# The mask phase of a two-layer cross-attention kernel with each chunk attended directly ahead of the next chunk's scores

## The reference

```python
xq = layer_norm(x, qn_w, qn_b)
ctx = layer_norm(context, cn_w, cn_b)
q = (xq @ q_w).reshape(B, N, H, D)               # H = 16 heads of D = 32
kv = (ctx @ kv_w).reshape(B, M, 2, H, D)
k, v = (kv[:, :, 0], kv[:, :, 1])
attn = jnp.einsum('bnhd,bmhd->bhnm', q, k) * scale
attn = jnp.where(xa_mask[:, None, :, :], neg, attn)
attn = jax.nn.softmax(attn, axis=-1)
out = jnp.einsum('bhnm,bmhd->bnhd', attn, v).reshape(B, N, C)
x = x + (out @ proj_w + proj_b)
```

## Time and profile before

| what | us |
|---|---|
| runs of the kernel before | median 2971.13 (2970.61 to 2973.69, 3 runs) |
| the profiled execution's own time | 2967.99 |
| its span, first to last instruction | 2965.3 |
| PE busy | 2803.9 (95%) |
| DVE busy | 1747.2 (59%) |
| ACT busy | 1632.9 (55%) |
| POOL busy | 631.0 (21%) |
| mean granted clock of PE | 0.980 of full |

### The profile page before, as it was taken

How to read it: one execution, slowest core, us unless ns; L and a number is a source line. 1 busy time by engine, 2 the same in 40 slices (tenths; PEclk the granted TensorE clock), 3 DMA queues, 4 the chain that set the end, 5 groups by cost and what they waited for, 6 DMA issues and landing times. The chain is left out here.

```text
span 2965.3 us, 69016 instructions
## 1 busy us (share of the span) xinstructions
PE 2803.9 (95%) x24864; PEld 2430.4 (82%) x24864; DVE 1747.2 (59%) x5357; ACT 1632.9 (55%) x4947; POOL 631.0 (21%) x773
## 2 busy tenths in 40 slices
PE   6999999996999999999899999995999999999995
PEld 6888888885888888888699998994888888888884
DVE  6666666664533332333367777775576767767674
ACT  6777777774311111111177777774666656656562
POOL 1110111021000000000012333332133324333233
PEclk9999999999999999999899999997999999999998
DMA  3111101111200000000211111113110011110100
GB/s 114 43 45 58 58 29 58 58 43 68 100 29 29 28 14 14 28 28 14 78 35 45 42 42 42 42 57 115 47 43 35 35 42 42 42 35 35 42 29 22
DMA packets 74804, 134.37 MB, mean 45 GB/s; under 512 B 10096, under 2 KB 10096, under 8 KB 74736
## 3 DMA queue, kind: packets, MB, share of 16 engines
q1 hardware_dynamic: 74736, 133.47, 13.0%
HBM read 99.90 MB, written 33.55 MB: 45 GB/s over the span
## 5 line engine op out<-in xcount | busy, mean ns | idle before, releaser
L1967 ACT ACTIVATE mlp_h<-mlp_f,mlp_b1col 128x512 f32<-128x512 f32 x128 | 88.3, 690 | 559.4 <-PE mlp_f L2091 559.3
L2027 DVE CAST mlp_hT_hi<-mlp_h 128x512 fp32r<-128x512 f32 x128 | 58.3, 455 | 440.0 <-ACT mlp_h L1967 440.0
L519 ACT ACTIVATE cross_prob<-cross_scores,cross_low 128x256 f32<-128x256 f32 x512 | 237.9, 492 | 14.1 <-DVE cross_low L897 14.1
L519 ACT ACTIVATE mask_prob<-mask_scores,mask_low 128x256 f32<-128x256 f32 x512 | 236.8, 475 | 11.3 <-DVE mask_low L903 10.3
L903 DVE CUSTOM_DVE_ANT_0 mask_scores<-mask_scores,mask_mask 128x256 f32<-128x256 f32 x512 | 201.5, 456 | 69.2 <-PE mask_scores L1296 68.7
L519 ACT ACTIVATE causal_prob<-causal_scores,causal_low 128x128 f32<-128x128 f32 (+1 forms) x512 | 211.1, 434 | 15.4 <-DVE causal_low L903 15.3
L2091 PE MATMUL mlp_f<-mlp_xT_hi,mlp_w_hi 128*128 128x512 f32 x512 | 200.2, 391 | 0.6 <-DVE mlp_xT_lo L2021 0.6
L2103 PE MATMUL mlp_acc<-mlp_w_hi,mlp_hT_hi 128*128 128x512 f32 x512 | 200.6, 392 | 0.0
L2091 PE MATMUL mlp_f<-mlp_xT_hi,mlp_w_lo 128*128 128x512 f32 x512 | 199.9, 391 | 0.0
L2091 PE MATMUL mlp_f<-mlp_xT_lo,mlp_w_hi 128*128 128x512 f32 x512 | 199.9, 390 | 0.0
L2103 PE MATMUL mlp_acc<-mlp_w_hi,mlp_hT_lo 128*128 128x512 f32 x512 | 199.4, 389 | 0.0
(11 more groups left out here) (333 smaller groups left out, 9394.4 us busy)
## 6 DMA issues: line engine op xcount, KB each, us to landing
mask_x_in<-in_x SPq DMA_DIRECT2D x16, 512.0 KB, 3.7
mask_c_in<-in_ctx SPq DMA_DIRECT2D x16, 512.0 KB, 5.2
mask_res<-in_x SPq DMA_DIRECT2D x16, 512.0 KB, 3.5
after_attention<-mask_res SPq DMA_DIRECT2D x16, 512.0 KB, 5.9
mlp_x<-after_attention SPq DMA_DIRECT2D x8, 1024.0 KB, 5.6
mlp_stage<-in_L_xattn_fc_w SPq DMA_DIRECT2D x8, 1024.0 KB, 5.0
after_layer<-mlp_y SPq DMA_DIRECT2D x8, 1024.0 KB, 4.2
causal_x_in<-after_layer SPq DMA_DIRECT2D x16, 512.0 KB, 4.1
```

The source lines that it names most:

```text
L519: ins = act.activation(prob[:, u % 4, qt, 0:w], SC[h][:, FROM[qt]:FROM[qt] + w], ACT.Exp, bias=low[:, u % 4, qt:qt + 1], scale=-1.0, accum ...
L1967: act.activation(h32[:, m % 2, :], F1[m % 2][:], ACT.Gelu, bias=b1col[:, m:m + 1]).then_inc(s["gelu"], 1)
L2027: dve.tensor_copy(hT[0][:, r, :], h32[:, r, :]).then_inc(s["h_hi"], 1)
```

## The change

It changes the order of the instructions in the mask phase on PE, ACT and DVE. Head 3 of a chunk is turned ahead of the second keys block (no longer in halves), `attend` follows keys and stands directly ahead of the next `scores`, and `attended` and the first turn of the new chunk follow the first block behind scores. Each later turn moves up by one block. In chunk 2 both `turn_over` calls stand together ahead of `queries(b + 1, 0)`. ACT's exponentials of a chunk and DVE's minima are no longer split by another instruction. `post_turn` of the second pair goes into SC[2] in place of O, so it waits for the exponentials of head 2, and scores wait for `post_lo`. The fourth matrix is split in turn 0 rather than in the prologue, and `qk_lo(b, 1)` on DVE goes to the end of the turn before. Twelve columns of indentation are taken off; "..." stands for chunk 3 of PE's turn, which follows the pattern of chunk 1 with the values of b+1 in place of the projection: attended(b, 2) and turn 12 behind the first half, then turn 13, queries half, turn 14, queries half, `post_turn(b, 0)`.

```diff
@@ -196,7 +196,7 @@
 T_BANK = (W1, O) if causal else (SC[2], SC[3], SC[2], SC[3])
 QK_BANK = W1 if cross else W0
 V_BANK = W0 if cross else W1
-POST_BANK = (W1, O) if cross else (SC[2], O)
+POST_BANK = (W1, O) if cross else (SC[2], SC[2])
 PT_BANK = (SC[0], SC[1], PT, PT)
@@ -567,42 +567,38 @@
 def mask_turn(b, prev, cur, nxt):
     if prev:
-        copy(b, -1)
-    if cur:
-        for u in (0, 1, 2):
+        attended(b, -1)
+    if cur:
+        for u in (0, 1, 2, 3):
             exps(b, u)
-    if prev:
-        attended(b, -1)
-    if cur:
-        exps(b, 3)
-        values(b, 1)
         copy(b, 0)
         copy(b, 1)
+        copy(b, 2)
     if prev:
         post_hi(b, 1)
-    if cur:
-        copy(b, 2)
+    elif cur:
+        matrix_hi(3)
+    if cur:
+        values(b, 1)
+        copy(b, 3)
         qk(b, 2)
-        copy(b, 3)
-        for u in (4, 5, 6):
+        attended(b, 0)
+        for u in (4, 5, 6, 7):
             exps(b, u)
-        attended(b, 0)
-        exps(b, 7)
         copy(b, 4)
         copy(b, 5)
+        copy(b, 6)
     if nxt:
         turned(b + 1, 0)
         turned(b + 1, 1)
     if cur:
-        copy(b, 6)
+        copy(b, 7)
         qk(b, 3)
-        copy(b, 7)
-        for u in (8, 9, 10):
+        attended(b, 1)
+        for u in (8, 9, 10, 11):
             exps(b, u)
-        attended(b, 1)
-        exps(b, 11)
         copy(b, 8)
     if nxt:
         turned(b + 1, 2)
@@ -610,22 +606,22 @@
     if cur:
         copy(b, 9)
         copy(b, 10)
+        copy(b, 11)
     if nxt:
         qk(b + 1, 0)
     if cur:
-        copy(b, 11)
-        for u in (12, 13, 14):
+        attended(b, 2)
+        for u in (12, 13, 14, 15):
             exps(b, u)
-        attended(b, 2)
-        exps(b, 15)
-    if nxt:
-        values(b + 1, 0)
-    if cur:
         copy(b, 12)
         copy(b, 13)
+        copy(b, 14)
+    if nxt:
+        values(b + 1, 0)
+    if cur:
         post_hi(b + 1, 0)
-        copy(b, 14)
+        copy(b, 15)
     if nxt:
         qk(b + 1, 1)
@@ -771,7 +767,6 @@
     matrix_hi(2)
     qk(0, 0)
     values(0, 0)
-    matrix_hi(3)
     qk(0, 1)
@@ -1014,51 +1009,48 @@
 def mask_turn(b, prev, cur, nxt):
     if cur:
-        minima(b, 0, (0, 1))
-        qk_lo(b, 1)
-        minima(b, 0, (2, 3))
+        minima(b, 0)
     if prev:
         attended(b, -1)
     if nxt:
         front(b + 1)
     if prev:
         post_lo(b, 1)
-    if cur:
-        minima(b, 1, (0, 1))
+    elif cur:
+        matrix_lo(3)
+    if cur:
         qk_lo(b, 2)
-        minima(b, 1, (2, 3))
+    if cur:
+        minima(b, 1)
+        attended(b, 0)
     if prev:
         project(b, 0)
-    if cur:
-        attended(b, 0)
     if nxt:
         turned(b + 1, 0)
         turned(b + 1, 1)
-    if cur:
-        minima(b, 2, (0, 1))
+    if cur:
         qk_lo(b, 3)
-        minima(b, 2, (2, 3))
+    if cur:
+        minima(b, 2)
+        attended(b, 1)
     if prev:
         project(b, 1)
     if nxt:
         turned(b + 1, 2)
         turned(b + 1, 3)
-    if cur:
-        attended(b, 1)
-    if cur:
-        minima(b, 3, (0, 1))
-    if nxt:
         qk_lo(b + 1, 0)
-    if cur:
-        minima(b, 3, (2, 3))
+    if cur:
+        minima(b, 3)
+        attended(b, 2)
     if nxt:
         mask_floats(b + 1)
     if cur:
-        attended(b, 2)
         post_lo(b + 1, 0)
+    if nxt:
+        qk_lo(b + 1, 1)
@@ -1192,7 +1184,7 @@
     matrix_lo(2)
     qk_lo(0, 0)
     mask_floats(0)
-    matrix_lo(3)
+    qk_lo(0, 1)
@@ -1406,145 +1398,122 @@
         if prev:
             pe.wait_ge(s["post_lo"], 2 * (b - 1) + 1)
         scores(b, 0)
-    if prev:
-        turn_probs(b, -1)
-    if cur:
         pe.wait_ge(s["v_ready"], 2 * b + 1)
         values(b, 1, 0)
-    if prev:
-        attend(b, -1)
-    if cur:
+    if prev:
+        attended(b, -1)
+    if cur:
+        turn_probs(b, 0)
         values(b, 1, 1)
-        turn_probs(b, 0)
-    if prev:
-        attended(b, -1)
-    if cur:
+        turn_probs(b, 1)
         pe.wait_ge(s["qk_lo"], KC * b + 2)
         queries(b, 2, 0)
-        turn_probs(b, 1)
+        turn_probs(b, 2)
         queries(b, 2, 1)
     if prev:
         pe.wait_ge(s["z_done"], KC * b + 1)
+        if cur:
+            scores_taken(b, 2)
         post_turn(b - 1, 1)
     if cur:
-        keys(b, 2, 0)
-        turned_free(b, 0)
-        turn_probs(b, 2)
-        keys(b, 2, 1)
+        turn_probs(b, 3)
+        keys(b, 2)
+        attend(b, 0)
+    if prev:
+        pe.wait_ge(s["post_lo"], 2 * b)
     if cur:
         scores(b, 1)
-        turn_probs(b, 3)
-    if prev:
-        pe.wait_ge(s["post_lo"], 2 * b)
+    if prev:
         pe.wait_ge(s["v_ready"], 2 * b + 2 if cur else 2 * B)
         project(b, 0, 0)
-    if cur:
-        attend(b, 0)
+    if cur:
+        attended(b, 0)
+        turn_probs(b, 4)
     if prev:
         project(b, 0, 1)
     if cur:
-        turn_probs(b, 4)
-    if cur:
-        attended(b, 0)
+        turn_probs(b, 5)
         pe.wait_ge(s["qk_lo"], KC * b + 3)
         queries(b, 3, 0)
-        turn_probs(b, 5)
+        turn_probs(b, 6)
         queries(b, 3, 1)
     if nxt:
         scores_taken(b, 6)
         turn_over(b + 1, 0)
         scores_taken(b, 7)
         turn_over(b + 1, 1)
     if cur:
-        keys(b, 3, 0)
-        turned_free(b, 1)
-        turn_probs(b, 6)
-        keys(b, 3, 1)
+        turn_probs(b, 7)
+        keys(b, 3)
+        attend(b, 1)
     if cur:
         if nxt:
             pe.wait_ge(s["t_act"], NP * (b + 1) + 2)
         scores(b, 2)
-        turn_probs(b, 7)
     if prev:
         pe.wait_ge(s["proj_read"], TT * (b - 1) + 2)
         project(b, 1, 0)
-    if cur:
-        attend(b, 1)
+    if cur:
+        attended(b, 1)
+        turn_probs(b, 8)
     if prev:
         project(b, 1, 1)
     if cur:
-        turn_probs(b, 8)
+        turn_probs(b, 9)
     if nxt:
         scores_taken(b, 10)
         turn_over(b + 1, 2)
+        scores_taken(b, 11)
+        turn_over(b + 1, 3)
+    if cur:
+        turn_probs(b, 10)
+    if nxt:
         pe.wait_ge(s["qk_lo"], KC * (b + 1))
         pe.wait_ge(s["t_lo"], NP * (b + 1) + 2)
         queries(b + 1, 0)
-        scores_taken(b, 11)
-        turn_over(b + 1, 3)
-    if cur:
-        turn_probs(b, 9)
-    if cur:
-        attended(b, 1)
+    if cur:
+        turn_probs(b, 11)
     if nxt:
         pe.wait_ge(s["t_lo"], NP * (b + 1) + 3)
         keys(b + 1, 0, 0)
-    if cur:
-        turned_free(b, 2)
-        turn_probs(b, 10)
-    if nxt:
         pe.wait_ge(s["t_lo"], NP * (b + 2))
         keys(b + 1, 0, 1)
+    if cur:
+        attend(b, 2)
...
-    if nxt:
-        keys(b + 1, 1, 0)
-    if cur:
-        turned_free(b, 3)
-        turn_probs(b, 14)
-    if nxt:
-        keys(b + 1, 1, 1)
+        turn_probs(b, 15)
+    if nxt:
+        keys(b + 1, 1)
+    if cur:
+        attend(b, 3)
```

More of the change, by code:

```diff
@@ L569, in mask_turn @@
                 if prev:
-                    copy(b, -1)
-                if cur:
-                    for u in (0, 1, 2):
-                        exps(b, u)
-                if prev:
                     attended(b, -1)
                 if cur:
-                    exps(b, 3)
-                    values(b, 1)
+                    for u in (0, 1, 2, 3):
+                        exps(b, u)
                     copy(b, 0)
                     copy(b, 1)
+                    copy(b, 2)
                 if prev:
                     post_hi(b, 1)
+                elif cur:
+                    matrix_hi(3)
                 if cur:
-                    copy(b, 2)
+                    values(b, 1)
+                    copy(b, 3)
                     qk(b, 2)
-                    copy(b, 3)
-                    for u in (4, 5, 6):
+                    attended(b, 0)
+                    for u in (4, 5, 6, 7):
                         exps(b, u)
-                    attended(b, 0)
-                    exps(b, 7)
                     copy(b, 4)
                     copy(b, 5)
+                    copy(b, 6)
                 if nxt:
@@ L616, in mask_turn @@
                 if cur:
-                    copy(b, 11)
-                    for u in (12, 13, 14):
+                    attended(b, 2)
+                    for u in (12, 13, 14, 15):
                         exps(b, u)
-                    attended(b, 2)
-                    exps(b, 15)
+                    copy(b, 12)
+                    copy(b, 13)
+                    copy(b, 14)
                 if nxt:
@@ L624, in mask_turn @@
                 if cur:
-                    copy(b, 12)
-                    copy(b, 13)
                     post_hi(b + 1, 0)
-                    copy(b, 14)
+                    copy(b, 15)
                 if nxt:
@@ L1415, in mask_turn @@
                 if prev:
-                    attend(b, -1)
-                if cur:
-                    values(b, 1, 1)
-                    turn_probs(b, 0)
-                if prev:
                     attended(b, -1)
```

(17 more changed lines are left out.)

## The result

| | before | after |
|---|---|---|
| median of 4 runs each, us | 2971.51 (2970.61 to 2973.69) | 3015.76 (3010.89 to 3016.80) |
| ratio | | 1.0145, interval 1.0127 to 1.0162 |
| profiled execution, us | 2967.99 | 3016.80 |
| its span, mean granted clock | 2965.3, 0.980 | 3014.9, 0.977 |

The change makes the kernel 1.5% slower. The forecast was 3008 us, range 2987 to 3024.

What follows compares the result with a forecast made beforehand. PE's own instruction order was taken to set the time (busy 42.78 of 43.00 us a turn). Loop 30.1, turn 0 5.0 and the end 1.9 summed to +37 us on the median 2971.13: 3008 us, range 2987 to 3024.

Steps and rivals of the forecast that it cites:

- (a): PE, each chunk: one change of array shape less, four to three; 0.15 us gained, 10 over 64 chunks.
- the unshown price: PE, attend directly followed by scores: taken as 1.00 us, bounds 0.11 less and 0.21 more.
- the walk: PE's instruction prices added through the new chunk 0 without any wait: 10.24 us against 10.39 before.
- (b): First turn of every chunk, 2.66 us behind scores, needs exponentials ready at 3.17: PE waits 0.51 us.
- The rival in which the gain comes through: First turn finds its exponentials ready, or waits were already counted: 1.3 us a turn gained, 2956 us; 7%.
- ACT's order: ACT's queued copies come late: attend in chunk 1 waits 0.35 us, turn 11 in chunk 2 waits 1.00.
- The rival with only the first wait: ACT's copies never late, chunks 1 and 2 both 11.15 us, turn 43.80: 2988 us; 13%.
- the rival with a further wait: DVE's qk_lo(b,3) late for chunk 2's minima: another 0.5 us a turn, attend's drain at upper bound, 3025 us; 12%.
- the loop's term: Mask phase loop: chunks add 0.36, 0.76, 0.67 and 0.36, +2.15 us a turn, +30 for 14 turns.
- Turn 0: First turn, with matrix_hi(3) moved in ahead of copy 3: 45.1 us against 40.13, +5.
- The end: Last turn's chunk 1 to the last projection 33.4 us against 31.86, +1.6; with its chunk 0, +1.9.
- the clock: Rival: PE falls from 2.4 to 1.2 GHz for whole turns, up to doubling its 42.78 us; 2%.

Runs made afterwards that it cites:

- e5: Changed kernel with the edits of e1, e2, e3 and e4 together; 2968.71 us, ratio 0.9981 to the kernel before.
- e1: Changed kernel with the first turn of each chunk moved behind the second half block, next to the second turn; 2999.50 us, ratio 1.0090 to before.
- e7: Changed kernel with chunk 0's first half block of values behind the first turn, not ahead of it; 3054.48 us, ratio 1.0270 to before.
- e3: Changed kernel with ACT's copy 7 put between the first and second turned piece of the next batch; 3009.49 us, ratio 1.0130 to before.
- e2: Changed kernel with head 3 turned into scores' bank 0, no longer sharing head 2's bank; 2997.76 us, ratio 1.0087 to before.
- e4: Changed kernel with the fourth matrix split in the prologue again; 3014.14 us, ratio 1.0143 to before.
- e6: e5 with banks for heads, turned inputs and outputs dealt out anew and the third piece ahead of chunk 2's first turn; 2966.47 us, ratio 0.9981.
- e8: e6 with ACT's copy 8 behind the fourth turned piece and turn 11 between the key halves in chunk 2; 2963.71 us, ratio 0.9970 to before.

## Why the prediction was right

**The gain of one change of shape, (a).** Right in size. Attend directly ahead of scores costs the same 1.00 as ahead of products. Both bounds of the unshown price (0.11 less, 0.21 more) proved unneeded. With the waits gone, e5 shows chunks 0 and 3 at 10.23 against the walk's 10.24. The kernel before has 10.39 there, 0.16 more, which would be 10 us over 64 chunks. That one change of shape less is what saves it is argued: no run changes the number of shape changes alone. The drain of the Trainium skill ("TensorE: Matmul & The Clock Gate", Single matmul latency) made 11 us of it, an estimate, and these 10 are near it.

**The wait of the first turn, (b).** Right: the turn starts 3.16 behind scores (3.16 to 3.18 in the loop turns, once 3.26) for the predicted 3.17, and the wait shows in 52 of 52 chunks. Of the hand-over of 0.05, for which the prediction had no row: the read that ends the head is over at 308.78 and PE turns at 308.83. e1 moves the turn and the wait goes; e7 moves it the other way and it still starts at 3.16. The rival in which the gain comes through decides at +2.66, and the exponentials are 0.5 too late for it.

**ACT's order.** Right in place and nearly in size: attend behind copy 7 (10.55 behind scores, predicted 10.50), turn 11 behind copy 10 (9.27, predicted 9.18). e3 and e2 undo one each and move one chunk each, by 0.34 and 0.79. The rival with only the first wait predicted 11.15 for chunks 1 and 2; they took 11.55 and 12.26. No `qk_lo` wait shows in the table, as the rival with a further wait would have it. (Its 3025 is mis-added: 3008, 14 x 0.5 and 13 for the drain make 3028. The high end by its own terms is 3025, and the chances of a slower kernel add to 91% where it says 89.)

**The size of the loop's term was low**, 30 for 33.2 us. The chunks came to 10.80, 11.55, 12.26 and 10.79 for the predicted 10.75, 11.50, 12.15 and 10.75. The four transposes that follow a wait take 0.41 (308.83 to 309.24), where I had the 0.36 of transposes behind products; that is 0.05 in each chunk. The prediction had it in its high bound, not in its sum. Chunk 2 has such a start twice and the copy 0.09 later than worked out.

**Turn 0** took 5.45 us more for the predicted 5.0: chunks 11.72, 10.68, 12.39, 10.79 for 11.55, 10.7, 12.15, 10.75.

**The end was the term mis-sized most**, +7.1 for +1.9, and most of that was the clock. Chunks 0, 1 and 2 of turn 15 gave 3.6 of it for the predicted 2.8 (10.77, 10.57 and 10.15 where before had 10.38, 9.87 and 7.63; predicted 10.27 and 9.66 for the last two). The other two parts are the stretch from the last scores to the projection and the projection. After, e4 with the same order, then before:

```profile
745.69:761.30 15.61, 9.71 (x72) 5.86 (x68) 5.66 (x22) 7.66 (x24) 2.50 (x2) 0.64 0.10 35
```

```profile
746.06:759.67 13.61, 7.68 (x72) 5.14 (x69) 5.66 (x22) 7.68 (x24) 2.50 (x2) 0.87 0.14 40
```

```profile
701.15:715.51 14.36, 7.77 (x89) 5.00 (x89) 5.80 (x22) 8.37 (x26) 2.50 (x2) 1.00 0.18 66
```

The prediction's 13.50 is what e4 shows (13.61), and e3 too (13.62). The changed kernel's profile has 15.61, 2.0 of it by the clock (0.64 for 0.87). The projection to mlp took 19.94 for 17.70 before, and 19.03 in e4. So the order itself costs some 3 us at the end, 1 more than predicted, and the lower clock some 4 in this profile. The prediction gave the clock 2%, as a fall for whole turns, and put the waits at 1.0 us at most. In the loop both held: from 120 to 640 us the granted clock was 1.00. It left out that in chunks 1 and 2 of turn 0 and in the last chunk no block of products stands behind scores, so that the first turn there waits 1.8 us. In the last turns the clock fell about 1 us behind such a wait (748.84; it was 0.50 from 749.9). Whether that wait alone brings it down is not shown: in the same place of turn 0 it did not, in this profile.

**Not in the sum at all** was 2.3 us of the prologue. PE's order up to the first scores is that of the kernel before; from ACT's and DVE's the fourth matrix is gone, and DVE has `qk_lo(0, 1)` in its place. The clock was 0.50 from 22.9 to 29.7 us in the profile of after, and near there in those of e1, e2, e4, e6, e7 and e8 (first scores at 32.5 to 33.9), but not in those of e3 and e5 (31.23 and 31.01). e4, e6 and e8, with the matrix back in the prologue, have it too, so the matrix is not its cause. It differs from run to run, and whether the change has a part in it stays open.

The median is 7.8 us above the forecast. In the profiles the misses add to more, 12.6 us: 3 in the loop, 0.5 in turn 0, 5 at the end, 2 in the prologue and 1.6 after the mask phase; the two profiled executions lie 48.8 us apart, the medians 44.3. All misses go the same way, so the sum owes nothing to errors that cancel. The prediction's statements that DVE's new order buys nothing and that `post_turn`'s new bank is hidden fit the tables, which have no such wait, but no run undoes either by itself.

## What to carry to other kernels

A reorder on the busiest engine that removes real work can still lose if it brings a consumer nearer to its producer. Read the distance from the start of the producer's chain to the consumer in both orders, here 5.39 and 2.66 against a chain of 3.17, before counting what is saved. Then walk the other engines' queues: ACT had 10 idle us a turn, and two of its copies were still late because they stood behind four pieces of the next sequence. Each such wait could be taken away by itself (a bank, an order on ACT, half a block on PE), and with most of them gone the same idea was worth 0.2 to 0.3%. Compare runs by stretch, too: the same order took 67.0 and 64.1 us in the last turns, and a gain of 0.9 us in turn 0 was hidden by a lower clock one chunk on. Where two waits follow each other in one chunk, as in chunk 2, taking away one gives back only part.

## What the runs showed of the hardware that was not expected

PE's clock fell after waits much shorter than I held to be harmless: in e7 a wait of 1.8 us behind 24 scores matmuls and two transposes, followed by four transposes, was followed by a granted clock of 0.65 in the mean over the next 4.87 us, with products 0.21 us apart in place of 0.12. Chunk 0 was lengthened so in 9 of 15 turns; in the other 6, with the same order and, in the turn shown, the same wait, the clock stayed at 1.00. Chunk 1 of turn 0 says the same across kernels: behind its wait of 1.8 us the clock fell in five profiles (e3, e4, e5, e6, e8) and stayed at 1.00 in four (after, e1, e2, e7). So the length of the wait alone does not decide it; what does, no run here shows. A wait of 1.0 us behind products, once in each loop turn of the changed kernel, left the clock at 1.00.

By the Trainium skill ("TensorE: Matmul & The Clock Gate", Part 4: PE-mode transpose), transposes do not count as busy for the clock in the same way as products. No run here tests that: in e7 the wait stands between the same transposes in the turns that fell and in those that did not.
